# Bias matmuls replaced by a bias in the PSUM evacuation, a third load slot in weight preparation, and a moved norm matmul

## The chip, the cores and the metric

One Trainium2 chip, eight cores. Every core runs the same program on its own two of the 16 sequences, and the cores do not exchange data. The time is that of the slowest core, in microseconds (us), for one execution.

## What is computed

One transformer layer for `t` of shape 16 x 4096 x 1024 in float32. Cut to what matters:

```python
xn  = layernorm(x)
qkv = xn @ W_qkv.T + b_qkv            # 3072 = Q, K, V of 1024 each; b_qkv has 3072 values
att = softmax(Q @ K.T / 32) @ V       # one head of 1024
x   = x + layernorm(att)
h   = silu(xn2 @ wg.T) * (xn2 @ wu.T) # xn2 = layernorm(x); wg, wu 3072 x 1024 int32 / 127
x   = x + layernorm(h @ wd.T)         # wd 1024 x 3072 int32 / 127
```

## The kernel before

The program emits every engine's instructions in a hand-written order, with semaphore waits between them. `P.em(engine, fn, waits, inc)` appends one; an engine runs its own in that order. Its parts are:

*Weight preparation* (`prep_chunk`, L170). All four weight matrices are loaded in 26 chunks (18 of 2 MB, 8 of 1.5 MB) by SP, cast to bf16 by ScalarE (L191), transposed by TensorE (L197), copied out of PSUM by VectorE (L203) and stored to HBM by GpSimd's queue (L210). There are two load slots in `varena` and two store slots `sstg`: chunk `ch` can be loaded once the casts of `ch - 2` are done, and staged once the store of `ch - 2` has landed. At its end the bias row is loaded and cast into `bq`, which lies in `kbufs` (L120, L237). A fence over all engines follows.

*Then, for each of two sequences:* phase 1 projects Q, K and V, phase 2 is attention, phase 3 the MLP. A fence ends the sequence.

*Phase 1* runs over 8 groups `g` of 512 tokens. The layer norm of a token tile (L134 to L143, L318) alternates between VectorE and ScalarE; those of group g+1 are emitted after QK steps 8, 10, 12 and 14 of group g, in the same two queues as the evacuations. A group then is:
- four tiles transposed into `LNxT` (L346, L354);
- 16 QK steps `e_`: eight matmuls of 128 x 512 into one of two `pqk` banks (L372) and a ninth, one-row matmul that adds the bias (`bq` slice as the stationary operand, `ones_row` moving, L376); ScalarE evacuates to bf16 (L385), VectorE squares (L396);
- after step 7 eight matmuls sum the squares of Q (`pqn`, L412), after step 15 those of K (`pkn`, L430), for a bound on the scores;
- V: four tiles x two halves, eight matmuls each into one of two `pv` banks (L458), a one-row bias matmul (L463) and ScalarE's evacuation into `varena` (L470);
- GpSimd's queue stores Q and K to HBM (L477, L487).

The weights come in six sets of 1 MB a group, w0 to w5, into two halves of `wbufs` (`wload`, L282). w0 to w3 serve four QK steps each. w0 and w1 are issued when the V stage before is done, w2 to w5 when the set two before has been used: w2 after step 3, w3 after step 7, w4 after step 11, w5 after step 15. V's first halves use w4, its second halves w5. All are issued by SP, in order; the four `t` tiles of group g+1 (L303, 512 KB each) are issued just behind w2. Q's store is issued after step 7.

*Phase 2* begins with a small chain on ScalarE, VectorE and TensorE (L493 to L511) that turns the norms into `bias_exp`. Blocks of 512 queries follow; K comes in sets of four tiles into two halves of `kbufs` (L645). The first K set of block 0 waits for the end of V, as `kbufs` holds the bias row (L649).

*At sequence 1's start* the bias row is loaded and cast again (L246 to L255), and the first four `t` loads wait for it (`bq_gate`).

## Time and profile before

| | |
|---|---|
| two timed executions | 5873.38 and 6515.4 us, median 6194.39 |
| the profiled execution | 5885.66 us; span of the slowest core 5884.1 |
| spans of the eight cores | 5850.5 to 5884.1 us |
| weight preparation | 0 to 284 us |
| phase 1, sequence 0 and 1 | 284 to 878 and 3079 to 3671 us |
| TensorE busy | 5042.6 us, 86% |
| VectorE, ScalarE, GpSimd busy | 1303.3, 1210.0, 221.3 us |
| mean granted TensorE clock | 0.93 |

The profile is one execution recorded by the hardware on its slowest core (core 2). Times in its rows are microseconds from the start of the span, means of one instruction are nanoseconds. PE is TensorE's matmuls, PEld its weight loads, DVE VectorE, ACT ScalarE, POOL GpSimd, SP the engine that issues loads. L372 is line 372 of the kernel. "[1.61 <-DMA ...]" behind an instruction is the idle time of its engine before it, and what ended it. Some matmul records are missing, so that x7 can stand for eight. A matmul's shown duration has its pipeline's tail in it; the distance of starts tells the rate.

### The profile page before, as it was taken

To read this page: it belongs to the slowest core of one execution; us is meant where nothing else is said; L and a number is where in the kernel's file an instruction comes from. 1 tells how busy PE (TensorE), PEld (TensorE's weight loads), DVE (VectorE), ACT (ScalarE), POOL (GpSimd) and SP (SyncE) were. 2 spreads that over 40 slices of the span, in tenths; PEclk is the share of its full clock that TensorE was granted. 3 is DMA by queue.
4 is the path that set the end of the run, shared out by engine and by line. 5 is a ranking of instruction groups with operands and counts; after the bars stand their busy time and mean duration, and the time that the engine had idled before them with its cause. 6 is when DMAs were issued, how large, how long until landed. Compare 5 with 4: busy or idle time off the path is not lost.

```text
span 5884.1 us, 59117 instructions; the slowest of 8 cores (5850.5 to 5884.1 us)
## 1 busy us (share of the span) xinstructions
PE 5042.6 (86%) x23063; PEld 2243.1 (38%) x23492; DVE 1303.3 (22%) x1908; ACT 1210.0 (21%) x1951; POOL 221.3 (4%) x310
## 2 busy tenths in 40 slices
PE   3388889999999698989888888999999969898988
PEld 2233334444444344444433333444444434444443
DVE  2232221111111222223223222111111122232322
ACT  3322222222122121212112222222212212121211
POOL 1100000000000000000000000000000000000000
PEclk6598999999999799999998999999999979999999
DMA  9855554444333533343325555444433353334332
GB/s 276 254 142 143 143 140 108 110 112 110 93 100 97 125 86 93 90 99 104 66 78 151 143 143 142 105 112 108 115 93 101 93 129 86 93 86 97 105 71 72
DMA packets 735510, 679.18 MB, mean 115 GB/s; under 512 B 409602, under 2 KB 655362, under 8 KB 734210
## 3 DMA queue, kind: packets, MB, share of 16 engines
q1 hardware_dynamic: 699748, 549.52, 38.4%
q0 software_dynamic: 35488, 125.85, 5.9%
q8 instruction: 191, 3.13, 0.2%
q14 instruction: 83, 0.68, 0.0%
HBM read 549.48 MB, written 125.83 MB: 115 GB/s over the span
## 4 chain that ended last, share of the span: by engine, by line
PE 75%; DMA 14%; DVE 4%; issue 3%; ACT 3%; SPq 0%; DVEq 0%; ACTq 0%; POOL 0%; POOLq 0%
PE s1pav L583 8%; PE s0pav L583 8%; PE s1pd L898 6%; PE s0pd L898 6%; PE s0psc L668 5%; PE s1psc L668 5%; DMA kbufs<-kscr 5%; PE s1pg L830 5%; PE s0pg L830 5%; PE s1pu L844 5%; PE s0pu L844 5%; DMA wbufs<-wqkvT 4%; PE s0pqk L372 4%; PE s1pqk L372 4%; PE s1pv L458 2%
## 5 line engine op out<-in xcount | busy, mean ns | idle before, releaser
L668 PE MATMUL s1psc<-qarena,kbufs 128*128 128x512 bf16 x2004 | 448.0, 380 | 40.7 <-DMA kbufs<-kscr 34.1
L668 PE MATMUL s0psc<-qarena,kbufs 128*128 128x512 bf16 x2004 | 447.2, 380 | 41.0 <-DMA kbufs<-kscr 31.2
L583 PE MATMUL s1pav<-varena,parena 128*128 128x512 bf16 x2005 | 456.8, 388 | 3.3 <-issue 1.4
L583 PE MATMUL s0pav<-varena,parena 128*128 128x512 bf16 x2005 | 450.4, 385 | 2.7 <-issue 0.6
L830 PE MATMUL s1pg<-varena,wbufs 128*128 128x512 bf16 x1504 | 353.0, 385 | 8.7 <-DVE varena L782 5.7
L830 PE MATMUL s0pg<-varena,wbufs 128*128 128x512 bf16 x1504 | 353.0, 385 | 8.7 <-DVE varena L782 5.7
L844 PE MATMUL s1pu<-varena,wbufs 128*128 128x512 bf16 x1504 | 344.8, 379 | 1.7
L844 PE MATMUL s0pu<-varena,wbufs 128*128 128x512 bf16 x1504 | 344.8, 379 | 1.7
L134 DVE BATCH_NORM_STATS2 stats<-evac 128x6 f32<-128x512 f32 x128 | 88.9, 694 | 1104.8 <-ACT evac L597 719.1
L668 PEld LDWEIGHTS s1psc<-qarena,kbufs 128*128 128x128 bf16 x2048 | 198.3, 98 | 289.0 <-issue 56.6
L668 PEld LDWEIGHTS s0psc<-qarena,kbufs 128*128 128x128 bf16 x2048 | 198.2, 98 | 288.6 <-issue 56.4
L583 PEld LDWEIGHTS s1pav<-varena,parena 128*128 128x128 bf16 x2048 | 203.9, 100 | 252.5 <-issue 22.3
L372 PE MATMUL s0pqk<-parena,wbufs 128*128 128x512 bf16 x992 | 254.3, 398 | 49.7 <-DMA wbufs<-wqkvT 42.9
L583 PEld LDWEIGHTS s0pav<-varena,parena 128*128 128x128 bf16 x2048 | 202.2, 99 | 247.2 <-issue 13.2
L372 PE MATMUL s1pqk<-parena,wbufs 128*128 128x512 bf16 x993 | 255.7, 400 | 43.9 <-DMA wbufs<-wqkvT 40.5
L197 PE MATMUL ptr<-ident,lnout 128*128 128x128 bf16 x768 | 92.2, 303 | 184.0 <-ACT lnout L191 141.0
L898 PE MATMUL s1pd<-varena,parena 128*128 128x512 bf16 x1008 | 232.3, 381 | 7.4 <-DVE qarena L864 6.5
L898 PE MATMUL s0pd<-varena,parena 128*128 128x512 bf16 x1008 | 230.6, 379 | 7.0 <-DVE qarena L864 6.2
L677 ACT ACTIVATE parena<-s1psc,bias_exp 128x512 bf16<-128x512 f32 x256 | 175.1, 687 | 293.8 <-PE s1psc L668 293.8
L677 ACT ACTIVATE parena<-s0psc,bias_exp 128x512 bf16<-128x512 f32 x256 | 175.1, 687 | 293.0 <-PE s0psc L668 293.0
L830 PEld LDWEIGHTS s1pg<-varena,wbufs 128*128 128x128 bf16 x1536 | 151.6, 99 | 195.2 <-issue 21.3
L830 PEld LDWEIGHTS s0pg<-varena,wbufs 128*128 128x128 bf16 x1536 | 151.5, 99 | 195.2 <-issue 21.4
(126 smaller groups left out, 4408.0 us busy)
## 6 DMA issues: line engine op xcount, KB each, us to landing
wbufs<-wgT SPq DMA_DIRECT2D x96, 512.0 KB, 4.4
wbufs<-wuT SPq DMA_DIRECT2D x96, 512.0 KB, 6.2
xa<-t SPq DMA_DIRECT2D x64, 512.0 KB, 7.2
xb<-t SPq DMA_DIRECT2D x64, 512.0 KB, 5.4
xnew<-evac POOLq DMA_DIRECT2D x64, 512.0 KB, 4.6
xa<-xnew SPq DMA_DIRECT2D x64, 512.0 KB, 7.7
xb<-xnew SPq DMA_DIRECT2D x64, 512.0 KB, 4.4
out<-evac POOLq DMA_DIRECT2D x64, 512.0 KB, 4.8
```

The costliest lines, as they stand in the source:

```text
L134: e.bn_stats(out=o, in_=i), waits=list(extra_waits), inc="dve")
L197: e.transpose(out=o, in_=i, identity=ident[:]),
L372: e.matmul(out=o, lhsT=l, rhs=rr, start=st, stop=False),
L458: e.matmul(out=o, lhsT=l, rhs=rr, start=st, stop=False),
L583: e.matmul(out=o, lhsT=l, rhs=rr, start=st, stop=sp),
L668: e.matmul(out=o, lhsT=l, rhs=rr, start=st, stop=sp),
L677: e.activation(out=o, in_=i, func=AF.Exp, scale=ISQ, bias=bias_exp[:]),
L830: e.matmul(out=o, lhsT=l, rhs=rr, start=st, stop=sp),
L844: e.matmul(out=o, lhsT=l, rhs=rr, start=st, stop=sp),
L898: e.matmul(out=o, lhsT=l, rhs=rr, start=st, stop=sp),
```

## The change

The bias matmuls are gone. At the end of weight preparation the Q and K part of the bias is loaded as 16 x 128, transposed into `bqT` (128 x 16), and the V part is spread over 128 partitions into `bvrep` by two matmuls. Q's and K's evacuation on ScalarE becomes an Identity activation with a per-partition bias; V's moves to VectorE as an add with `bvrep`. The bias is not loaded again for sequence 1, no `t` load waits for it, and the first K load doesn't wait for V. The K norm's matmuls and its two small VectorE operations move from behind step 15 to behind the two halves of V's first tile. Weight preparation has three load slots, and its two store slots move from `varena` to `qarena`.

```diff
-    bq = kbufs[0:1, 0:E3]
+    bqT = sb("bqT", [128, 16], F32)
+    bvrep = sb("bvrep", [128, 1024], F32)
...
-    sstg = varena[:, 32768 - 16384: 32768]
+    sstg = qarena
...
-        slot = ch % 2
+        slot = ch % 3
         lsrc = vf32[:, slot * 4096: slot * 4096 + nsub * 1024]
         if in_i32:
             lsrc = lsrc.bitcast(I32)
-        lsem = ("wla", "wlb")[slot]
+        lsem = ("wla", "wlb", "qa")[slot]
         lt = (lsem, P.em(syn, lambda e, o=lsrc.rearrange(
                   "p (c d) -> p c d", c=nsub), i=src_ap:
                   e.dma_start(out=o, in_=i),
-                  waits=[("act", cast_tok.get(ch - 2)), ("pool", init_tok)],
+                  waits=[("act", cast_tok.get(ch - 3)), ("pool", init_tok)],
                   inc=lsem, amt=16))
         ld_tok[ch] = lt
-        stg = sstg[:, slot * 4096: slot * 4096 + nsub * 1024]
+        stg = sstg[:, (ch % 2) * 4096: (ch % 2) * 4096 + nsub * 1024]
...
-        psem = ("psa", "psb")[slot]
+        psem = ("psa", "psb")[ch % 2]
...
-    bqf = parena.bitcast(F32)[0:1, 0:E3]
-    bl = ("misc", P.em(syn, lambda e: e.dma_start(out=bqf,
-                                         in_=bqkv.rearrange("(a e) -> a e", a=1)),
-              inc="misc", amt=16))
-    bq_tok = P.em(act, lambda e: e.activation(out=bq[:], in_=bqf, func=AF.Copy),
-                  waits=[bl], inc="act")
+    pbv = [pps.enter_context(nc.psum_tensor(f"pbv{i}", [128, 512], F32))
+           for i in range(2)]
+    bstg = parena.bitcast(F32)[0:16, 0:128]
+    bstg2 = parena.bitcast(F32)[0:1, 1024:2048]
+    b16 = lnout[0:16, 0:128]
+    b16v = lnout[0:1, 1024:2048]
+    bl = ("misc", P.em(syn, lambda e: e.dma_start(
+        out=bstg, in_=bqkv[0:2048].rearrange("(c p) -> c p", p=128)),
+        inc="misc", amt=16))
+    blv = ("misc", P.em(syn, lambda e: e.dma_start(
+        out=bstg2, in_=bqkv[2048:3072].rearrange("(a e) -> a e", a=1)),
+        inc="misc", amt=16))
+    c1 = P.em(act, lambda e: e.activation(out=b16, in_=bstg, func=AF.Copy),
+              waits=[blv, ("pe", tr_tok[sub_i[0] - 2]), ("pool", init_tok)],
+              inc="act")
+    c2 = P.em(act, lambda e: e.activation(out=b16v, in_=bstg2, func=AF.Copy),
+              waits=[blv, ("pe", tr_tok[sub_i[0] - 1])], inc="act")
+    bt = P.em(pe, lambda e: e.transpose(out=ptr[0][:, 0:16], in_=b16,
+                                        identity=ident[0:16, 0:16]),
+              waits=[("act", c1), ("dve", cp_tok[sub_i[0] - 2])], inc="pe")
+    bm0 = P.em(pe, lambda e: e.matmul(out=pbv[0][:, :], lhsT=ones_row[0:1, 0:128],
+                                      rhs=b16v[:, 0:512], start=True, stop=True),
+               waits=[("act", c2)], inc="pe")
+    bm1 = P.em(pe, lambda e: e.matmul(out=pbv[1][:, :], lhsT=ones_row[0:1, 0:128],
+                                      rhs=b16v[:, 512:1024], start=True, stop=True),
+               inc="pe")
+    bq_tok = P.em(act, lambda e: e.activation(out=bqT[:], in_=ptr[0][:, 0:16].bitcast(F32)[:, 0:16] if False else ptr[0][:, 0:16], func=AF.Copy),
+                  waits=[("pe", bt)], inc="act")
+    P.em(act, lambda e: e.activation(out=bvrep[:, 0:512], in_=pbv[0][:, :],
+                                     func=AF.Copy), waits=[("pe", bm1)])
+    bq_tok = P.em(act, lambda e: e.activation(out=bvrep[:, 512:1024],
+                                              in_=pbv[1][:, :], func=AF.Copy),
+                  inc="act")
...
-        if s > 0:
-            bqf2 = xa.bitcast(F32)[0:1, 0:E3]
-            bl2 = ("misc", P.em(syn, lambda e, o=bqf2,
-                                in2=bqkv.rearrange("(a e) -> a e", a=1):
-                                e.dma_start(out=o, in_=in2),
-                                inc="misc", amt=16))
-            bq_tok = P.em(act, lambda e, o=bq, i=bqf2:
-                          e.activation(out=o, in_=i, func=AF.Copy),
-                          waits=[bl2], inc="act")
-            bq_gate = ("act", bq_tok)
-        else:
-            bq_gate = ("act", bq_tok)
+        bq_gate = None
...
-                waits=[apply_tok.get(tile - 4), dbg_gate.get(tile - 2),
-                       bq_gate if tile < 4 else None],
+                waits=[apply_tok.get(tile - 4), dbg_gate.get(tile - 2)],
...
-                          ("act", bq_tok)]
+                          ("act", bq_tok if g == 0 else None)]
+                mmt = None
                 for c in range(8):
                     lhs = wv[:, (e_ % 4) * 1024 + c * 128:
                              (e_ % 4) * 1024 + (c + 1) * 128]
                     rhs = LNxT[:, c * 512:(c + 1) * 512]
-                    P.em(pe, lambda e, o=pqk[bank][:, :], l=lhs, rr=rhs, st=(c == 0):
-                         e.matmul(out=o, lhsT=l, rhs=rr, start=st, stop=False),
-                         waits=mwaits if c == 0 else ())
-                mmt = P.em(pe, lambda e, o=pqk[bank][:, :],
-                           l=bq[:, e_ * 128:(e_ + 1) * 128], rr=ones_row[:, :]:
-                           e.matmul(out=o, lhsT=l, rhs=rr, start=False, stop=True),
-                           inc="pe")
+                    mmt = P.em(pe, lambda e, o=pqk[bank][:, :], l=lhs, rr=rhs,
+                               st=(c == 0), sp=(c == 7):
+                               e.matmul(out=o, lhsT=l, rhs=rr, start=st, stop=sp),
+                               waits=mwaits if c == 0 else (),
+                               inc="pe" if c == 7 else None)
                 if e_ < 8:
                     dst = QTst[:, e_ * 512:(e_ + 1) * 512]
                     stage_free = qt_dma.get(g - 1)
                 else:
                     dst = Kst[:, (e_ - 8) * 512:(e_ - 8 + 1) * 512]
                     stage_free = kscr_dma.get(g - 1)
-                et = P.em(act, lambda e, o=dst, i=pqk[bank][:, :]:
-                          e.activation(out=o, in_=i, func=AF.Copy),
+                et = P.em(act, lambda e, o=dst, i=pqk[bank][:, :],
+                          b=bqT[:, e_: e_ + 1]:
+                          e.activation(out=o, in_=i, func=AF.Identity, bias=b),
                           waits=[("pe", mmt), stage_free], inc="act")
...
-                if e_ == 15:
-                    tok = None
-                    for c in range(8):
-                        tok = P.em(pe, lambda e, o=pkn[:, :],
...
-                              ("act", vql_tok.get((g, j - 1, hf),
-                                                  vql_tok.get((g - 1, 3, hf)))),
-                              ("act", bq_tok)]
+                              ("dve", vql_tok.get((g, j - 1, hf),
+                                                  vql_tok.get((g - 1, 3, hf))))]
+                    mmt = None
                     for c in range(8):
                         lhs = LNxT[:, c * 512 + j * 128: c * 512 + (j + 1) * 128]
-                        P.em(pe, lambda e, o=pv[hf][:, :], l=lhs,
-                             rr=wv4[:, :, c, :], st=(c == 0):
-                             e.matmul(out=o, lhsT=l, rhs=rr, start=st, stop=False),
-                             waits=mwaits if c == 0 else ())
-                    mmt = P.em(pe, lambda e, o=pv[hf][:, :],
-                               l=ones_row[:, 0:128],
-                               rr=bq[:, 2048 + hf * 512: 2048 + (hf + 1) * 512]:
-                               e.matmul(out=o, lhsT=l, rhs=rr,
-                                        start=False, stop=True),
-                               inc="pe")
+                        mmt = P.em(pe, lambda e, o=pv[hf][:, :], l=lhs,
+                                   rr=wv4[:, :, c, :], st=(c == 0), sp=(c == 7):
+                                   e.matmul(out=o, lhsT=l, rhs=rr,
+                                            start=st, stop=sp),
+                                   waits=mwaits if c == 0 else (),
+                                   inc="pe" if c == 7 else None)
                     dst = varena[:, tile * 1024 + hf * 512:
                                  tile * 1024 + (hf + 1) * 512]
                     vql_tok[(g, j, hf)] = P.em(
-                        act, lambda e, o=dst, i=pv[hf][:, :]:
-                        e.activation(out=o, in_=i, func=AF.Copy),
-                        waits=[("pe", mmt)], inc="act")
+                        dve, lambda e, o=dst, i=pv[hf][:, :],
+                        b=bvrep[:, hf * 512:(hf + 1) * 512]:
+                        e.tensor_add(out=o, in0=i, in1=b),
+                        waits=[("pe", mmt)], inc="dve")
+                if j == 0:
+                        tok = None
+                        for c in range(8):
+                            tok = P.em(pe, lambda e, o=pkn[:, :],
+                                       rr=q2s[:, c * 512:(c + 1) * 512],
+                                       st=(c == 0), sp=(c == 7):
+                                       e.matmul(out=o, lhsT=ones_col[:], rhs=rr,
+                                                start=st, stop=sp),
+                                       waits=[("dve", sq2_tok[(g, 15)]),
+                                              ("dve", kmax_tok.get(g - 1))],
+                                       inc="pe" if c == 7 else None)
+                        kn_tok[g] = tok
+                        rm = P.em(dve, lambda e, i=pkn[:, :]: e.reduce_max(
+                            out=tiny[:, 6:7], in_=i, axis=AX.X),
+                            waits=[("pe", tok)], inc="dve")
+                        kmax_tok[g] = P.em(dve, lambda e: e.tensor_max(
+                            out=tiny[:, 1:2], in0=tiny[:, 1:2], in1=tiny[:, 6:7]),
+                            waits=[("dve", rm)], inc="dve")
...
-                  waits=[("dve", nb_), ("act", vql_tok[(NG1 - 1, 3, 0)])],
+                  waits=[("dve", nb_), ("dve", vql_tok[(NG1 - 1, 3, 0)])],
...
-                               ("ksr", ks_relay[si]),
-                               ("pe", vlast_tok[NG1 - 1]
-                                if (b == 0 and si == 0) else None)],
+                               ("ksr", ks_relay[si])],
```

## Rows read from the trace of the kernel before

**Rows 1.** The page's chain that ended last, by engine, share of the span.
```profile
PE 75%; DMA 14%; DVE 4%; issue 3%; ACT 3%; SPq 0%; DVEq 0%; ACTq 0%; POOL 0%; POOLq 0%
```
**Rows 2.** Groups by line: bias matmuls. Columns: count | busy us, mean ns | idle before.
```profile
L376 PE MATMUL s0pqk<-ones_row,kbufs 1*128 1x512 bf16 x128 | 50.4, 394 | 1.2
L463 PE MATMUL s0pv<-kbufs,ones_row 1*128 1x512 bf16 x64 | 24.8, 388 | 0.0
```
**Rows 3.** Timeline, PE: two bias matmuls in phase 1, one score set. Columns: start, us.
```profile
311.52 0.39 PE L376 MATMUL s0pqk<-ones_row,kbufs 1*128 1x512 bf16 x1
...
313.67 0.39 PE L376 MATMUL s0pqk<-ones_row,kbufs 1*128 1x512 bf16 x1
...
918.69 7.07 PE L668 MATMUL s0psc<-qarena,kbufs 128*128 128x512 bf16 x31 [0.88 <-ACT parena L677]
```
**Rows 4.** Timeline, PE, group 6 of sequence 0 and the start of group 7.
```profile
741.82 3.19 PE L372 MATMUL s0pqk<-parena,wbufs 128*128 128x512 bf16 x7 [5.22 <-DMA wbufs<-wqkvT]
...
762.38 1.89 PE L412 MATMUL s0pqn<-q2s,ones_col 128*1 128x512 bf16 x8 [1.37 <-DVE q2s L396]
...
774.48 1.89 PE L372 MATMUL s0pqk<-parena,wbufs 128*128 128x512 bf16 x8 [1.61 <-DMA wbufs<-wqkvT]
...
785.86 1.89 PE L430 MATMUL s0pkn<-q2s,ones_col 128*1 128x512 bf16 x8 [2.73 <-DVE q2s L396]
...
790.42 1.89 PE L458 MATMUL s0pv<-wbufs,parena 128*128 128x512 bf16 x8 [0.52 <-DMA wbufs<-wqkvT]
...
813.74 3.19 PE L372 MATMUL s0pqk<-parena,wbufs 128*128 128x512 bf16 x7 [5.52 <-DMA wbufs<-wqkvT]
```
**Rows 5.** Chain that ended last, weight loads in order of time. Columns: issue, us.
```profile
761.15 13.08 DMA wbufs<-wqkvT
783.27 7.02 DMA wbufs<-wqkvT
...
3413.13 11.92 DMA wbufs<-wqkvT
```
**Rows 6.** Windows of group 6: each engine's busy time, granted clock, DMA share, GB/s.
```profile
742.00:747.00 5.00, 5.00 (x14) 1.48 (x13) 0.43 (x1) 0.60 (x1) 0.00 (x0) 0.57 0.61 119
754.00:772.00 18.00, 16.53 (x70) 6.10 (x71) 6.00 (x14) 4.57 (x9) 0.91 (x1) 1.00 0.97 289
...
794.00:807.00 13.00, 12.52 (x65) 4.94 (x63) 0.82 (x2) 3.58 (x6) 0.00 (x0) 1.00 0.01 2
```
**Rows 7.** Timeline, PE: the K norm of group 0.
```profile
349.95 3.16 PE L430 MATMUL s0pkn<-q2s,ones_col 128*1 128x512 bf16 x8 [2.73 <-DVE q2s L396]
```
**Rows 8.** Timeline, SP: the issue of the `t` tiles in group 6.
```profile
753.32 5.73 SPq L303 DMA_DIRECT2D xa<-t  x4
```
**Rows 9.** Timeline, PE: from the last V matmul to the first scores.
```profile
880.36 0.35 PE L507 MATMUL s0pv<-tiny,ones_rf 1*128 1x1 f32 x2 [2.00 <-DVE tiny L504]
887.10 15.05 PE L668 MATMUL s0psc<-qarena,kbufs 128*128 128x512 bf16 x62 [6.40 <-DMA kbufs<-kscr]
```
**Rows 10.** Groups by line: an add, two evacuations, table loads at the Ln line.
```profile
L925 DVE TENSOR_TENSOR evac<-dn,xb 128x1024 f32<-128x1024 f32 x64 | 78.4, 1226 | 12.1 <-DVE dn L920 12.1
...
L677 ACT ACTIVATE parena<-s0psc,bias_exp 128x512 bf16<-128x512 f32 x256 | 175.1, 687 | 293.0 <-PE s0psc L668 293.0
...
L385 ACT ACTIVATE parena<-s0pqk 128x512 bf16<-128x512 f32 x128 | 75.9, 593 | 247.7 <-PE s0pqk L376 247.7
...
L140 ACT ACT_TABLE_LOAD x26 | 33.4, 1283 | 88.7 <-DVE stats L138 88.7
```
**Rows 11.** Chain that ended last, start of sequence 1. Columns: start, us.
```profile
3078.90 1.94 DMA xa<-bqkv
3080.92 2.77 ACT kbufs L253
```
**Rows 12.** Windows of weight preparation, columns as in rows 6.
```profile
0.00:40.00 40.00, 11.59 (x96) 9.38 (x96) 8.20 (x12) 13.33 (x13) 5.12 (x15) 1.00 0.80 244
40.00:220.00 180.00, 63.23 (x520) 50.37 (x520) 43.36 (x63) 66.41 (x66) 28.29 (x17) 0.56 0.97 287
220.00:284.00 64.00, 17.42 (x152) 14.20 (x152) 13.92 (x21) 21.07 (x19) 9.94 (x7) 0.53 0.75 222
```

More of the change, by code:

```diff
@@ L423, in build_nc @@
                         waits=[("dve", rm)], inc="dve")
-                if e_ == 15:
-                    tok = None
-                    for c in range(8):
-                        tok = P.em(pe, lambda e, o=pkn[:, :],
-                                   rr=q2s[:, c * 512:(c + 1) * 512],
-                                   st=(c == 0), sp=(c == 7):
-                                   e.matmul(out=o, lhsT=ones_col[:], rhs=rr,
-                                            start=st, stop=sp),
-                                   waits=[("dve", sq2_tok[(g, 15)]),
-                                          ("dve", kmax_tok.get(g - 1))],
-                                   inc="pe" if c == 7 else None)
-                    kn_tok[g] = tok
-                    rm = P.em(dve, lambda e, i=pkn[:, :]: e.reduce_max(
-                        out=tiny[:, 6:7], in_=i, axis=AX.X),
-                        waits=[("pe", tok)], inc="dve")
-                    kmax_tok[g] = P.em(dve, lambda e: e.tensor_max(
-                        out=tiny[:, 1:2], in0=tiny[:, 1:2], in1=tiny[:, 6:7]),
-                        waits=[("dve", rm)], inc="dve")
             for j in range(4):
```

## The prediction

> **What bounds the kernel now.** I read the chain that ended last first: three quarters of the span are TensorE's own work and a seventh is DMA [rows 1]. TensorE is the engine to follow, but only where it is not waiting. The groups by line then give the size of what is removed: 384 one-row bias matmuls, 256 into `pqk` and 128 into `pv`, each shown at about 0.39 us [rows 2]. Busy time is not what one costs, since matmuls overlap, so I take starts. In projection phase one `e_` step of eight matmuls plus bias repeats every 2.15 us (311.52 to 313.67), while 32 matmuls of the score phase, which have no bias, take 7.07 us with a tail of 0.38, that is 0.216 us each [rows 3]. Eight of them are 1.73 us, so one bias matmul costs 0.42 us, twice a full matmul: both changes between one-row and 128-row weights break the overlap. In all 384 x 0.42 = 162 us of TensorE time go. The question is how much of that was free to go, and that is read from one group of the projection phase.
>
> I call T the first QK matmul of group 6 of sequence 0, at 741.82 us [rows 4]; w0 to w5 are its six 1 MB weight loads into two buffers. Each of w2 to w5 starts when the set two before it is used up. Today: T+19.2 QK step 7 ends; T+22.4 step 8 starts after the Q norm; step 12 waits 1.61 us for w3; step 15 ends at T+41.3; 2.73 us of wait, the K norm (1.8 us), the first V half; the second V half waits for w5 until T+48.6; V ends 7 x 2.15 us later, T+63.8; the next group starts at 813.74, T+71.9 [rows 4]. The loads: w3 goes out at 761.15 and takes 13.08 us (11.92 in a group of sequence 1), w5 goes out at 783.27 and takes 7.02 us [rows 5]. Between 754 and 772 us the DMA engines are 97% busy (w2, four tiles of `t`, w3, the Q store); in the V stage they are idle [rows 6]. So w3 is bound by bandwidth and w5 by latency, and neither gets shorter with faster matmuls.
>
> The clock: the granted clock is 0.57 of full in the first 5 us of the group [rows 6], after 5.2 us of idle PE. After 2.73 us of idle the K norm took 1.89 us in this group but 3.16 us in group 0 [rows 4, 7], so such a wait sometimes leads to half clock; after 1.37 us [rows 4] it did not here. Half clock is 0.43 us a matmul, so 5 us of it lose 2.5 us of matmuls without bias (today 2.0, the steps' gaps hide in it).
>
> **The change, part by part.** *Groups 0 to 6, both sequences (14).* New times: step 3 ends T+9.4 (11.7 matmuls in the slow 5 us, 20.3 at 0.216), step 7 T+16.3, step 8 starts 3.2 us later as now, T+19.5, step 11 ends T+26.4. Bounds of w3: its own duration, T+16.3 + 11.9 = T+28.2; or bandwidth, 20.9 us after the `t` loads start (753.32 to 774.23 today [rows 5, 8]), which is T+10.2 + 20.9 = T+31.1. I take the middle, so step 12 starts at T+29.9: a wait of 3.5 us. Four steps 6.9 us, and the price of the clock after such a wait between 0 and 2.5, taken 1.3 as it is near the 2.73 us waits: step 15 ends at T+38.1. Now the moved K norm: it no longer fills the wait for w5. w5 is there 7.3 us after step 15 as today, T+45.4, and only one V half (1.7 us) stands before it, so PE idles 5.6 us, a wait as long as those with a sure low clock. Then seven V halves 12.1, the K norm 1.8, low clock 2.5: V ends T+61.8. The way to the next group stays 8.1 us (w0 can be loaded only when V ends): T+69.9 against 71.9. That is 2.0 us a group, 28 us in all. With both prices at their good end (w3 at 28.2, no low clock after it) it is 4.6 a group, 64 us; at their bad end (31.3 for step 12, 2.5) the group takes 72.5 us, a loss of 8 us in all.
>
> *Group 7 (2).* No `t` is loaded, so w3 is there in time: step 15 ends T+33.3, V starts in earnest at T+40.6, V ends T+57.0, against 878.36 - 813.74 = 64.6 [rows 4, 9]. I take 6 of those 7.6 us for each, since w5 shares the engines with Q and now K loads: 12 us, bounds 8 and 15.
>
> *V's evacuation on VectorE, Q and K's with a bias.* The trace has no such add; the f32 add of 1024 columns took 1.23 us, so 512 lie between half of that, 0.61, and all of it, and I take 0.65 us, as the columns are half. ScalarE's copy took 0.59, its activation with bias and scale 0.69 [rows 10]; one with a bias alone lies between. All are hidden behind a 1.73 us V half or step; VectorE is otherwise empty in the V stage. Even at 1.23 us an add fits into the V half beside it. I cost it at nothing; without that cover it would be 0.65 us for each of 128 adds, 83 us.
>
> *Projection to scores (2).* Without the bias row in `kbufs`, the first two K loads no longer wait for V and land under it. Today V's end 878.36, the softmax bias matmul 880.36, then 6.40 us until K at 887.10, and the first 64 score matmuls take 15.05 us where 64 x 0.216 is 13.8 [rows 9]. What stays is the chain 2.0 + 0.35 + about 1.4 us for ScalarE's copy of `bias_exp` with its two hand-overs (an estimate, twice an activation of 0.69): 3.8 instead of 8.7, and part of the 1.1 us of clock. 5.5 each, 11 us (8 to 15). The third K load still waits for a buffer.
>
> *Start of sequence 1.* The reload of the bias goes: 1.94 us DMA and 2.77 us ScalarE, in series ahead of `t` [rows 11]. 5 us.
>
> *Weight preparation.* Three load slots instead of two. DMA engines are busy 80% in the first 40 us, 97% up to 220 us and 75% at the end [rows 12]. A third load fills the first hole: 0.20 x 40 = 8 us, less the 3 us before any load, 5 us. In the middle it brings nothing. At the end the two store slots, untouched, limit it. Lower bound of the gain 0; upper 5 plus 0.25 x 64 = 16, 21 us. I take 5. The new transposes and copies of the bias lie under the last store.
>
> Sum: 28 + 12 + 11 + 5 + 5 = 61 us off 5885.7 us (the profiled execution, span 5884.1): **5825 us**, -1.0%. Bounds: -8 + 8 + 8 + 5 + 0 = 13 to 64 + 15 + 15 + 5 + 21 = 120 us. The median of the two runs shown, 6194.39, is a mean of two far apart, 5873.38 and 6515.4; the profiled execution is near the lower and I forecast on its level.
>
> The Trainium skill (TensorE: Matmul & The Clock Gate, back-to-back issue gap) gives a 512-column matmul about 216 ns and says that the number of rows of a weight load does not matter. The spacing without bias agrees; the 0.42 us of the bias matmul does not. By the page's figure 83 us would go raw: V and steps 12 to 15 would save 2.4 us a group less, the 14 groups would lose 6 us instead of gaining 28, the last ones would gain 2 instead of 12, and the sum would be 17 us, 5869 us.
>
> **Rivals.** (a) *Both new waits cost the full clock price.* 3.5 us is longer than the waits that were sometimes free and shorter than those never free. With w3 also at its bandwidth bound: groups +8 instead of -28, 5861 us. For it: the 97%; against: w3 took 1.2 us less in sequence 1. The same page (HAM oscillation) says that DMA waits between bursts of matmuls bring every burst back to half clock; the trace agrees for the 5.2 us waits and not for 1.37 us. By the page alone with my middle w3, 1.2 us a group more, 5842 us.
> (b) *TensorE-bound after all*: loads come as early as the matmuls ask. Then all 162 us go, with 11 + 5 + 5: 5703 us. For it: step 12 waited for w3 only 1.61 us. Against: the 97% and the latency of w5.
> (c) *Slower*: ScalarE must switch function tables between the new biased evacuation and Ln/Exp of the next layer norms. A load is 1.283 us and there were 26 at the Ln line [rows 10], too few for one at each layer norm, so Copy shares a table with them; nothing in the trace shows that Identity does. If not: two loads at each of four layer norms, 10.3 us a group, less the 3.5 us of wait it hides in: 6.8 x 14 = 95 us, 5920 us. It decides once a layer norm loses more than 2 us. The Trainium skill (ScalarE: Activation LUTs, Table sets) counts identity among the functions that every set holds, which speaks against (c).
> (d) *Preparation gains its bound*, 21 instead of 5: 5809 us, inside my range.
>
> **Chances.** My case with (d) 0.62, (a) 0.21, (b) 0.07, (c) 0.06, others 0.04. The range 5775 to 5875 us takes in the bounds 120 and 13 us and holds the first two. A measurement of this kernel can tell about 2%, 118 us. Faster by more: (b) and one of the others, 0.08. Slower by more (6003 us): 0.03, as (c) alone stays below. Within: 0.89.
>
> **What would show it.** QK steps 1.73 us apart at full clock; step 12 waiting 2 to 5 us for w3 in groups 0 to 6 and hardly in 7; about 5.6 us of wait for w5 before the second V half of every group, and a low clock after it; groups 68 to 72 us apart; TensorE's 384 one-row matmuls gone but its idle time up by about 100 us; no table load between layer norms; scores within 4 us of V's end; first `t` load right after the fence. Wrong would be a wait for w5 below 3 us, groups 65 us apart, or V halves spaced by VectorE.

## The result and the profile after

The changed kernel took 5811.04 us in its profiled execution, 74.6 us less than the one before (5885.66). Over all executions the medians are 5938.89 us (11 runs, 5805.93 to 6361.35) against 6342.86 us (10 runs); they say little, since in about half of the executions of every kernel the cores of one die or of both ran at a lower granted clock, and only the others are compared in this document, except for the length of weight preparation, for which all profiled ones are used. Those compared lie, for the changed kernel, between 5805.93 and 5812.79 us, and the ratio to before is 0.9878 [0.9858, 0.9898]: 1.2% less time, which is under the 2% that a measurement of this kernel can tell.

Part of the 74.6 us belongs to the profiled execution of before. Measured again later, next to the experiments, before took 5858.55 to 5875.37 us in eleven of the twelve executions compared (5923.94 in the other). In the first of these series it took 5867.6 us in the mean of three, and the changed kernel with two load slots 5808.9 us in the mean of two, ratio 0.9896 [0.9842, 0.995]: 59 us, near the 61 of the forecast.

The page of after, in order: the span, the engines' busy time, the chain that ended last by engine.

```profile
span 5809.5 us, 58400 instructions; the slowest of 8 cores (5776.5 to 5809.5 us)
...
PE 4930.9 (85%) x22697; PEld 2243.9 (39%) x23111; DVE 1387.4 (24%) x2036; ACT 1151.7 (20%) x1826; POOL 221.2 (4%) x310
...
PE 71%; DMA 16%; DVE 4%; issue 3%; ACT 3%; SPq 1%; DVEq 0%; ACTq 0%; POOL 0%; POOLq 0%
```

TensorE's share of the chain fell from 75 to 71%, DMA's rose from 14 to 16% [rows 1]: the time was partly handed from matmuls to weight loads. The groups by line of after say where (columns as in rows 2):

```profile
L390 PE MATMUL s0pqk<-parena,wbufs 128*128 128x512 bf16 x1000 | 248.2, 408 | 72.0 <-DMA wbufs<-wqkvT 59.6 <-ACT parena L401 8.7 <-DVE parena L370 1.4
L390 PE MATMUL s1pqk<-parena,wbufs 128*128 128x512 bf16 x1000 | 248.0, 407 | 68.3 <-DMA wbufs<-wqkvT 51.6 <-ACT parena L401 13.5 <-ACT stats L141 1.2
...
L455 PE MATMUL s0pv<-wbufs,parena 128*128 128x512 bf16 x512 | 127.7, 409 | 44.8 <-DMA wbufs<-wqkvT 44.8
...
L401 ACT ACTIVATE parena<-s0pqk,bqT 128x512 bf16<-128x512 f32 x128 | 86.4, 683 | 376.2 <-PE s0pqk L390 376.2
...
L464 DVE TENSOR_TENSOR varena<-s0pv,bvrep 128x512 bf16<-128x512 f32 x64 | 44.2, 691 | 110.3 <-PE s0pv L455 110.3
...
L141 ACT ACT_TABLE_LOAD x26 | 33.4, 1283 | 88.6 <-DVE stats L139 88.6
```

The same two groups of sequence 0 before:

```profile
L372 PE MATMUL s0pqk<-parena,wbufs 128*128 128x512 bf16 x992 | 254.3, 398 | 49.7 <-DMA wbufs<-wqkvT 42.9 <-ACT parena L385 1.9 <-ACT stats L143 1.5
...
L458 PE MATMUL s0pv<-wbufs,parena 128*128 128x512 bf16 x512 | 125.7, 390 | 4.9 <-DMA wbufs<-wqkvT 4.9
```

The V matmuls, which waited 4.9 us in all for weights before, wait 44.8 now; the QK matmuls wait 59.6 us for weights, 42.9 before. V's add on VectorE is hidden: no V matmul waits for it. ScalarE's evacuation of Q and K is not: the QK matmuls wait for it (L401) 8.7 us in sequence 0 and 13.5 in sequence 1, where 1.9 and 0 stood before. The table loads at the layer norm's line are still 26 [rows 10].

By stages, each line the profiled execution of before and of after (from starts in the two traces), and what the prediction's sum had for it:

| stage | before, us | after, us | gained | forecast |
|---|---|---|---|---|
| weight preparation, to the first `t` load | 284.2 | 275.5 | 8.7 | 5 |
| groups 0 to 6, both sequences | 1010.6 | 991.6 | 19.0 | 28 |
| group 7 to the first scores, both | 145.4 | 117.9 | 27.5 | 12 + 11 |
| phase 3 of sequence 0 and start of sequence 1 | 1156.3 | 1151.9 | 4.4 | 5 |
| attention, both | 2128.0 | 2115.8 | 12.2 | 0 |
| first `t` load to first QK, and the last phase 3 | 1159.6 | 1156.8 | 2.8 | 0 |
| sum | 5884.1 | 5809.5 | 74.6 | 61 |

Phase 1, from its first QK matmul to the first scores, in four sums that I worked out of the traces (the length; TensorE's idle time in waits over 0.15 us; the time in which it worked at half clock, 1.2 of 2.4 GHz; and "work", the length less the idle time and half of the half-clock time), in us, sequence 0 / sequence 1:

| kernel | length | idle | at half clock | work |
|---|---|---|---|---|
| before | 580.9 / 575.0 | 96.0 / 88.7 | 56.1 / 59.2 | 456.9 / 456.8 |
| after | 557.0 / 552.5 | 133.1 / 130.0 | 86.2 / 82.4 | 380.7 / 381.4 |

The work removed is 76.2 + 75.4 = 151.6 us, near the 162 us foreseen for the bias matmuls. Of it 78 us came back as idle time and 27 us (half of 30.1 + 23.2) as half clock; 46 us stayed. Of the idle time 20 us are waits for ScalarE's evacuations (22.2 against 1.9).

One group shows how. This is PE's timeline in group 6 of sequence 0 of after, the group of rows 4:

```profile
725.24 16.12 PE L390 MATMUL s0pqk<-parena,wbufs 128*128 128x512 bf16 x62 [4.93 <-DMA wbufs<-wqkvT]
742.82 1.89 PE L427 MATMUL s0pqn<-q2s,ones_col 128*1 128x512 bf16 x8 [1.46 <-DVE q2s L412]
...
751.10 1.89 PE L390 MATMUL s0pqk<-parena,wbufs 128*128 128x512 bf16 x7 [1.11 <-ACT parena L401]
755.35 5.34 PE L390 MATMUL s0pqk<-parena,wbufs 128*128 128x512 bf16 x24 [2.36 <-DMA wbufs<-wqkvT]
761.46 1.89 PE L390 MATMUL s0pqk<-parena,wbufs 128*128 128x512 bf16 x8 [0.77 <-ACT parena L401]
763.19 1.89 PE L455 MATMUL s0pv<-wbufs,parena 128*128 128x512 bf16 x8
770.63 3.57 PE L455 MATMUL s0pv<-wbufs,parena 128*128 128x512 bf16 x8 [5.56 <-DMA wbufs<-wqkvT]
774.14 1.99 PE L472 MATMUL s0pkn<-q2s,ones_col 128*1 128x512 bf16 x8
...
795.38 4.84 PE L390 MATMUL s0pqk<-parena,wbufs 128*128 128x512 bf16 x15 [6.04 <-DMA wbufs<-wqkvT]
```

and these are its loads w3, w5 and the next w0, from the chain that ended last, with the window around w3 (columns of rows 6):

```profile
741.86 13.25 DMA wbufs<-wqkvT
763.49 7.01 DMA wbufs<-wqkvT
786.73 8.03 DMA wbufs<-wqkvT
```

```profile
738.00:755.00 17.00, 12.32 (x54) 4.91 (x54) 7.42 (x16) 5.48 (x11) 0.91 (x1) 1.00 1.02 306
```

w3 went out 16.6 us after T (19.3 before) and took 13.25 us (13.08 before [rows 5]) with the DMA engines fully busy; w5 took 7.01 (7.02). Neither got shorter, so TensorE, which is now done with w2 sooner, waits at step 12 (755.35), and the second V half waits 5.56 us where 0.52 us stood before. The eight matmuls behind that wait are shown with 3.57 us, half clock, where the eight of the first V half have 1.89. Steps 11 and 15 (751.10 and 761.46) wait 1.11 and 0.77 us for ScalarE's evacuation.

### The profile page after: what moved, and what is told of

It reads as the page before. It is cut to its first block, busy times and chain, and to the rows that moved or that the text cites. A ratio compares the mean times of both kernels' runs of the same rounds, so it can differ in the third digit from the quotient of the medians.

```text
span 5809.5 us, 58400 instructions; the slowest of 8 cores (5776.5 to 5809.5 us)
## 1 busy us (share of the span) xinstructions
PE 4930.9 (85%) x22697; PEld 2243.9 (39%) x23111; DVE 1387.4 (24%) x2036; ACT 1151.7 (20%) x1826; POOL 221.2 (4%) x310
## 4 chain that ended last, share of the span: by engine, by line
PE 71%; DMA 16%; DVE 4%; issue 3%; ACT 3%; SPq 1%; DVEq 0%; ACTq 0%; POOL 0%; POOLq 0%
PE s0pav L596 8%; PE s1pav L596 8%; DMA wbufs<-wqkvT 6%; PE s0pd L909 6%; PE s1pd L909 6%; PE s0psc L679 6%; DMA kbufs<-kscr 5%; PE s0pg L841 5%; PE s1pg L841 5%; PE s0pu L855 5%; PE s1pu L855 5%; PE s1psc L679 5%; PE s0pqk L390 3%; PE s1pqk L390 3%; PE s0pv L455 2%
## 5 line engine op out<-in xcount | busy, mean ns | idle before, releaser
L679 PE MATMUL s0psc<-qarena,kbufs 128*128 128x512 bf16 x2004 | 446.3, 379 | 26.0 <-DMA kbufs<-kscr 16.3
L596 PE MATMUL s0pav<-varena,parena 128*128 128x512 bf16 x2005 | 458.5, 389 | 3.3 <-issue 1.2
L390 PE MATMUL s0pqk<-parena,wbufs 128*128 128x512 bf16 x1000 | 248.2, 408 | 72.0 <-DMA wbufs<-wqkvT 59.6
L596 PEld LDWEIGHTS s1pav<-varena,parena 128*128 128x128 bf16 x2048 | 204.1, 100 | 252.9 <-issue 23.2
```

What stands on the lines that cost most here:

```text
L390: e.matmul(out=o, lhsT=l, rhs=rr, start=st, stop=sp),
L596: e.matmul(out=o, lhsT=l, rhs=rr, start=st, stop=sp),
L679: e.matmul(out=o, lhsT=l, rhs=rr, start=st, stop=sp),
```

## Experiments

**The K norm back behind step 15.** Of the change everything is kept but the K norm's move.

```diff
+                if e_ == 15:
+                    ... (K norm: 8 matmuls, reduce_max, tensor_max)
...
-                if j == 0:
-                    ... (the same)
```

> The changed kernel with one part undone: the K norm's matmuls and its two VectorE operations stand behind QK step 15 again, ahead of V. Theory (the second V half waits for w5, 7.3 us after step 15, whatever stands before it): the norm's 1.8 us go back into that wait, V ends 1.8 us earlier in each of 16 groups, and the wait of 5.6 us falls apart into about 2.7 and 1.1 us, so that the low clock after it costs 1.3 instead of 2.5 us: 3 us a group, 48 us in all, 5763 us. Rival (the move paid, since it took the wait of 2.73 us for the last square out of TensorE's way): 2.7 us a group come back, 5854 us.

Measured: 5751.4 and 5750.2 us, ratio to before 0.9797 [0.9755, 0.9839]. PE's timeline of this kernel in the group that starts at 621.37:

```profile
657.67 1.89 PE L390 MATMUL s0pqk<-parena,wbufs 128*128 128x512 bf16 x8 [0.77 <-ACT parena L401]
662.29 1.89 PE L446 MATMUL s0pkn<-q2s,ones_col 128*1 128x512 bf16 x8 [2.73 <-DVE q2s L412]
664.11 1.90 PE L474 MATMUL s0pv<-wbufs,parena 128*128 128x512 bf16 x8
666.72 12.25 PE L474 MATMUL s0pv<-wbufs,parena 128*128 128x512 bf16 x56 [0.71 <-DMA wbufs<-wqkvT]
```

From the start of step 15 to the second V half it is 666.72 - 657.67 = 9.05 us here and 770.63 - 761.46 = 9.17 us in after: w5 sets this moment in both. But here the K norm lies in front of it, and in after behind it, with the half clock that follows 5.56 us of idle. The V stage from then on: 678.80 - 666.72 = 12.1 us against 786.43 - 770.63 = 15.8 us (to the first transposes, 678.80 and 786.43 in the two timelines). That is 3.7 us in this group. Over all 16, phase 1 is 524.8 / 532.0 us long here and 557.0 / 552.5 in after, 52.7 us or 3.3 a group; the kernels differ by about 60, and the rest of it lies outside phase 1, where single executions differ by as much. So the move of the K norm cost over 50 us, more than the whole change gained in phase 1 (46).

**Idle matmuls in the wait for w5.** 22 matmuls of `ones_col` with `LNxT` into the `pkn` bank, whose result is overwritten, behind the first V half.

```diff
+                    if j == 0 and hf == 0:
+                        for f_ in range(22):
+                            P.em(pe, ... e.matmul(out=pkn, lhsT=ones_col[:], rhs=rr,
+                                          start=True, stop=True), ...)
```

> The changed kernel with 22 idle matmuls (one column of ones by 512 columns, into the K norm's bank, overwritten after) behind the first V half of each group, in the wait of 5.6 us for w5. They take 4.8 us at full clock and compute nothing that is used. Theory (a wait of 5.6 us is followed by about 5 us at half clock, which costs 2.5 us): the wait stays as long but TensorE is busy in it, and the clock stays up: 2 us a group, 32 us in all, 5779 us. Rival (the clock behind the wait costs nothing, or the fillers themselves run at half clock and come out of the wait late): 5811 us or more.

Measured: 5782.4 and 5780.6 us, about 29 us below after. Phase 1: length 540.3 / 540.9, idle 94.0 / 94.8, half clock 48.8 / 47.5, work 421.9 / 422.3. PE's timeline of this kernel:

```profile
675.02 4.91 PE L470 MATMUL s0pkn<-parena,ones_col 128*1 128x512 bf16 x22
680.48 1.89 PE L455 MATMUL s0pv<-wbufs,parena 128*128 128x512 bf16 x8 [0.55 <-DMA wbufs<-wqkvT]
```

The second V half comes no sooner, 680.48 - 671.48 = 9.0 us after step 15's start, but what follows runs at full clock. The clock's share of the wait for w5 is thus about 2 us a group, which the prediction had as 2.5; what is left of the 3.3 us a group is near the 1.8 us of the K norm's own matmuls.

**Four weight buffers instead of two.** `xb` and `evac`, idle in phase 1, become buffers 3 and 4, so that each load is issued two sets earlier. In after and in before:

```diff
+        def wbuf(gs):
+            i = gs % 4
+            if i < 2:
+                return wbufs[:, i * 4096:(i + 1) * 4096]
+            return (xb, evac)[i - 2].bitcast(BF16)[:, 0:4096]
...
-                    wload(g, e_ // 4 + 2)
+                    wload(gs + 4)
```

> The changed kernel with four buffers for the weight sets of phase 1 instead of two: xb and evac, idle in that phase, hold the third and fourth, and a set is loaded as soon as the set four before it is used up. Theory (the waits for w0, w3 and w5 and the low clock behind them eat what the bias matmuls gave): the waits go, a group takes TensorE's own 49 us and 3 us of layer norms in the way, 52 instead of 71, and the kernel about 290 us less, 5520 us (5480 to 5600). Rival (DMA bandwidth is the bound, not the two buffers): groups stay above 65 us, 5720 us or more.

> The kernel before, with bias matmuls, the K norm behind step 15 and two slots in preparation, with the same four buffers. Theory (a bias matmul costs 0.42 us of TensorE and its removal is hidden only by the loads): with loads out of the way the change is worth its full 384 x 0.42 = 162 us plus 9 in preparation and 10 at the borders, so this kernel is about 180 us above the changed one with four buffers, near 5700 us. Rival (a bias matmul costs 0.216 us like any other): 83 + 19 us above it, near 5620 us.

Measured: after with four buffers 5565.7, 5562.7, 5557.0 us, ratio to before 0.9472 [0.9429, 0.9514]; before with four buffers 5769.3, 5766.2 us, ratio 0.9826 [0.9784, 0.9868]. PE's timeline of a whole group of the first:

```profile
508.53 15.66 PE L393 MATMUL s0pqk<-parena,wbufs 128*128 128x512 bf16 x64 [1.16 <-DVE parena L374]
525.65 1.89 PE L430 MATMUL s0pqn<-q2s,ones_col 128*1 128x512 bf16 x8 [1.46 <-DVE q2s L415]
527.47 5.35 PE L393 MATMUL s0pqk<-parena,xb 128*128 128x512 bf16 x24
...
543.34 3.62 PE L457 MATMUL s0pv<-wbufs,parena 128*128 128x512 bf16 x16
546.88 1.89 PE L474 MATMUL s0pkn<-q2s,ones_col 128*1 128x512 bf16 x8
548.71 10.53 PE L457 MATMUL s0pv<-wbufs,parena 128*128 128x512 bf16 x48
```

No wait for a weight load is left, and its groups by line have none over the whole sequence (the line of the first and third set):

```profile
L393 PE MATMUL s0pqk<-parena,wbufs 128*128 128x512 bf16 x512 | 120.0, 395 | 9.1 <-ACT parena L404 4.6 <-DVE parena L374 4.5
```

The next group starts at 563.14, 54.6 us later, and between 507 and 562 us the DMA engines are 73% busy. Phase 1: with the change 433.3 / 433.8 us, work 382.4 / 382.3; without it 527.3 / 523.0, work 458.5 / 458.9. So the same change that brings 74 us with two buffers brings 5767.8 - 5564.2 = 204 us with four (spans of the profiled executions). This is the main evidence for the theory of the forecast, that the loads' return times and not the matmuls set a group; the 204 are somewhat above the 180 expected. Phase 1 gives 94.0 + 89.2 = 183 of them, its way to the scores included: 153 of work, 4 of half clock and 26 of idle time (50.7 / 50.2 without the change, 37.3 / 37.6 with it). The last is the balance of three things: 41 us of waits in front of the K norm and 12 us for the first K loads are gone, and TensorE waits 21 us for ScalarE's evacuations, 0 without the change. So moving the K norm may well pay with four buffers, where it cost with two; no run has its old place with four.

**Three buffers** (only `xb` added).

> The changed kernel with three buffers for the weight sets instead of two or four (xb is the third). Theory (what hurts is that a set's load can start only when the set two before it is done, not the bandwidth): with three, w0 of the next group and w5 are asked for one set earlier and are there in time, and the kernel is within 20 us of that with four, 5570 to 5590 us. Rival (a set behind the four t tiles needs more than 12 us, and three buffers still leave TensorE waiting for it): 2 to 5 us a group remain, 5600 to 5650 us.

Measured: 5557.6 us, one execution, as with four. By it one more load in flight is enough.

**What a ninth matmul costs when nothing waits.** The kernel with four buffers gets a ninth matmul of zeros in every QK step and V half, with 128 rows or with one; the result is not altered.

```diff
+    zt = sb("zt", [128, 128], BF16)          # zeros
...
+                mmt = P.em(pe, lambda e, o=pqk[bank][:, :], l=zt[0:ROWS, :],
+                           rr=LNxT[0:ROWS, 0:512]:
+                           e.matmul(out=o, lhsT=l, rhs=rr, start=False, stop=True),
+                           inc="pe")
```

> The changed kernel with four weight buffers (5565.7 us), with a ninth matmul added to each of the 384 accumulations of phase 1: stationary operand 128 rows x 128 columns of zeros, moving operand 128 x 512. It adds nothing to the result. Theory (what doubled the price of a bias matmul was the change between one row and 128 rows): it costs 0.216 us, 83 us in all, 5649 us, steps 1.94 us apart. Rival (a ninth matmul with another kind of operand costs 0.42 us whatever its rows): 5728 us, 2.15 us apart.

> As the run before, but the ninth matmul has one row (a row of 128 zeros stationary, one row of 512 moving), as the bias matmuls had. Theory: 0.42 us each, steps 2.15 us apart, 162 us in all, 5728 us. Rival (rows don't matter): same as with 128 rows, 5649 us.

Measured, one execution each: 5628.2 us with 128 rows and 5689.2 us with one row, against 5557 to 5566 without. PE's timelines, first with 128 rows, then with one (its core 0):

```profile
300.37 0.38 PE L399 MATMUL s0pqk<-parena,zt 128*128 128x512 bf16 x1
...
302.31 0.38 PE L399 MATMUL s0pqk<-parena,zt 128*128 128x512 bf16 x1
```

```profile
301.86 0.38 PE L399 MATMUL s0pqk<-parena,zt 1*128 1x512 bf16 x1
...
304.01 0.38 PE L399 MATMUL s0pqk<-parena,zt 1*128 1x512 bf16 x1
```

The same durations are shown, but the steps are 1.94 and 2.15 us apart, where eight matmuls alone take 1.73: the ninth costs 0.21 us with 128 rows and 0.42 us with one. The second is the spacing of before [rows 3]. Over 384 of them these are 81 and 161 us; the time rose by about 65 and 126 us. The difference is seen in phase 1. With 128 rows its work rose by 81 us, while the half-clock time fell from 27.3 / 27.8 to 8.0 / 19.4 us, worth half of that, 14 us, and the idle time by 10. With one row (core 0) the work rose by 153 us, while the half-clock time fell to 9.7 / 14.6 us, worth 15, and the idle time by 22. Nearly all of the idle time that went was waiting for ScalarE's evacuations: 21.1 us with steps of 1.73 us, 11.5 with 1.94 and 0.7 with 2.15, the same Identity activation in all three. So it is the shorter step that ScalarE, which does layer norms between the evacuations, cannot keep up with.

**Weight preparation.** The change without the third slot; before with the two store slots moved to `qarena`; before with that and the third slot. These and before were run again for the spread.

```diff
-        slot = ch % 3          # the first: back to ch % 2, cast_tok.get(ch - 2)
+        slot = ch % 2
...
-    sstg = varena[:, 32768 - 16384: 32768]     # the second, in before
+    sstg = qarena
```

> The changed kernel with two load slots in weight preparation, as before; all else stays. Theory (the third slot gave the 8.7 us by which the first t load is earlier, all of it in the first 40 us and the last 60): the first t load at 284 us instead of 275.5, 5820 us. Rival (the 8.7 us came from elsewhere, such as the bias row that no longer has its cast at the end): first t load stays at 275.5, 5811 us.

> The kernel before with only the change in weight preparation: three load slots, and the two store slots in qarena instead of varena. Phase 1 keeps its bias matmuls and the bias row. Theory one (the third slot, or the new place of the store slots, gave the 8.7 us by which the first t load is earlier): first t load near 270 us, 5872 us. Theory two (the difference is in the bias row's cast, or it is the spread between executions): first t load at 275 to 284 us as in the two profiles of the old preparation, 5881 us.

> The kernel before with only the two store slots moved from varena to qarena; two load slots. If the place of the store slots is what counts, the first t load comes near 265 us, as in the changed kernel with two slots, 5870 us. If the third slot counts, it stays at 275 to 284 us, 5881 us. If neither does, this kernel, the one with three slots and the one before lie within 5 us of each other on the mean of the cores.

> The changed kernel with two load slots in weight preparation, profiled a second time. Its first profile had the first t load at 265.0 us on the mean of the cores, 257.7 on one die. Theory (the third slot is worth about 8 us and that one die was a stray of this execution): mean 272 to 276 us. Rival (two slots are as good as three once the store slots are in qarena and the bias has its new cast): 264 to 267 us.

> The kernel before, unchanged, profiled a second time for the spread of weight preparation between executions. Theory (the 283.4 us of its first profile, mean of the cores, is the upper end of a spread): first t load at 274 to 277 us. Rival (the old place of the store slots costs 8 us more): 280 to 284 us.

> The kernel before with the store slots in qarena and two load slots, profiled again. If its 274.6 us for the first t load (mean of the cores) is its own, it comes at 273 to 276 us again; if two slots are as good as three, near 266.

> The kernel before with the whole new weight preparation (three load slots), profiled again. If the third slot is worth 8 us in this program, 265 to 268 us for the first t load; if the difference to the run before it is the spread of an execution, anything between 264 and 276.

> The changed kernel with two load slots, profiled a third time. After 265.0 and 267.1 us: if two slots with the new bias cast are as good as three, 264 to 268 us again; if those were strays, 272 to 276 us.

Measured: without the third slot 5803.7, 5814.0 and, again, 5801.9 us (after: 5806 to 5813), not the 5820 of the theory. Before with its store slots moved 5861.1, 5864.0, 5862.3, 5859.2 and 5861.75 us, ratio 0.9979 [0.9919, 1.0039]; with the third slot too 5855.35 us, from its second run; its first, before's second and the third of after with two slots gave only their preparation. The start of the first `t` load, the mean over the eight cores of one profiled execution, is a finer measure (each value is one execution of one kernel with this preparation):

| kernel | two load slots | three load slots |
|---|---|---|
| with the bias handling of before | 283.4 (before), 274.9, 274.6, 275.7, 273.7 | 266.5, 267.0 |
| with that of after | 265.0, 267.1, 270.7 | 270.9 (after), 264.1, 264.3, 266.7, 264.8, 266.5, 266.4 |

The second profiles of before (275.7), of before with its store slots moved (273.7), of that with three slots (267.0) and of after with two (267.1) came where one of the two expectations had them; the third of after with two, 270.7, fell between both. In before the third slot is worth 7 to 8 us; in after it is worth nothing that these runs can tell, though executions of one kernel differ by 6 to 8 us (265.0 to 270.7; before 283.4 and 275.7). With two slots the kernels with the new bias handling are 7 us sooner in the mean than those with the old (283.4 left out), which is about what the third slot brings alone, and the two don't add up. The end of preparation, where the bias is handled, does not make that difference: the last weight load already goes out at 245.4 to 246.5 us (mean over the cores; 253.2 in the profile of before) with the old and at 237.4 to 242.9 with the new, and up to there the instructions are the same. The cast of the bias row was hidden, too: in the profile of before it ends at 274.1 us, the last store is issued at 277.5 and the first `t` load at 284.2. What made the kernels with the new bias handling faster up to there is open. In the windows view of after the first 40 us are now 92% full and the middle 98% (80 and 97% before [rows 12]):

```profile
0.00:40.00 40.00, 12.51 (x104) 10.15 (x104) 8.20 (x12) 15.33 (x15) 5.69 (x15) 1.00 0.92 276
40.00:220.00 180.00, 61.87 (x515) 49.66 (x515) 43.87 (x65) 65.47 (x65) 27.72 (x17) 0.72 0.98 299
```

A third load in flight mostly lengthened each: the median 2 MB load took 27 us where it had taken 17.8.

## Where the prediction was right, and the step that failed

The mechanism was right: in groups 0 to 6 TensorE waits for w3 and w5 and most of the bias matmuls' time comes back as waits and half clock. The step that failed is "Four steps 6.9 us" with the evacuations "at nothing": TensorE waits for ScalarE's evacuations, and groups 0 to 6 gained 19 us, not 28. The times compared, 5806 to 5813 us, lie in the range and 12 to 19 us below 5825. The median over all executions, 5938.89 us, lies above it: "I forecast on its level" left the forecast without any term for the executions above that of the profile. The sum was 61 and 74.6 us were gained, but that the two are as near as that is partly luck: the 9 us too many in groups 0 to 6 are outweighed by 12.2 us in attention, in which the change has hardly a part, 4.5 at the border to the scores, 3.7 in preparation and 2.8 in places without a term. The sentence that the range takes in the bound of 120 us is off: 5885.7 - 120 is 5766, below 5775. Step by step:

*The timetable of group 6* came out within 0.6 us at nearly every point: step 7's end T+16.1 (16.3 forecast), step 12's start T+30.1 (29.9), step 15's end T+38.0 (38.1), the wait for w5 5.56 (5.6) up to T+45.4 (45.4), V's end T+61.2 (61.8), next group T+70.1 (69.9). Step 12's wait was 2.36 us and not 3.5, since step 11 had already waited 1.11 us for ScalarE, whose evacuation came late among the layer norms. The two bounds for w3 (T+28.2 and T+31.1) were both right as a pair: it landed at T+28.3 to T+31.3 over the groups.

*Groups 0 to 6: 28 forecast, 19 measured. The failed step in numbers.* In the mean of the 14 groups step 12 starts at T+30.1 (29.9 forecast), V follows 8.64 us later (8.2), w5's V half 7.47 after that (7.3) and the next group 24.6 later (24.5): a period of 70.8 us, 0.9 above the forecast, while before's mean was 72.2, 0.3 above the 71.9 taken. The largest part is the stretch from step 12 to V. Its matmuls are the 6.9 us of the forecast and its half clock 2.35 us, a price of 1.2 where 1.3 was taken; the rest is mostly 0.46 us of waiting for ScalarE's evacuations, 6 us over the 14 groups, where the forecast had nothing. The price of the clock was right as a mean of two kinds of groups: in nine of the ten that waited for w3 TensorE then ran at half clock for about 3.4 us (5.9 in one), and in group 6 of sequence 0, after 2.36 us, and in the four that waited at step 12 for something else, 1.2 to 2.1 us, it did not. So rival (a), the full price after both waits, came true for w5's wait and half true for w3's. The Trainium skill (TensorE: Matmul & The Clock Gate, HAM oscillation) has every burst behind a DMA wait of its kernel come back at half clock, a price of 2.5 here by the forecast; the trace agrees for the waits for w5 and for nine of the ten for w3. The periods, 68.4 to 73.8 us, are spread wider than the forecast's one number.

*The wait for w5* was foreseen with its cause, 5.35 to 5.87 us in groups 0 to 6, and the experiment with the K norm moved back shows what moving it cost, 53 us in phase 1. The forecast held the move's effect inside the 2.0 us a group and never set it apart. Had it, its own timetable would have shown that this one part of the change costs a group (1.8 us of norm and part of the 2.5 us of clock) more than the whole change brings it.

*Group 7 and projection to scores: 23 forecast, 27.5 measured.* The chain was as described. PE's timeline of after:

```profile
852.91 0.35 PE L520 MATMUL s0pv<-tiny,ones_rf 1*128 1x1 f32 x2 [1.54 <-DVE tiny L517]
854.09 13.76 PE L679 MATMUL s0psc<-qarena,kbufs 128*128 128x512 bf16 x62 [0.84 <-ACT bias_exp L524]
```

The scores start 1.18 us after the softmax bias matmul, where 6.74 us stood before [rows 9] and 0.35 + 1.4 were estimated, and the first 64 take 13.8 us, at full clock. ScalarE's copy with its two hand-overs took 0.84 us, not 1.4. In group 7 w5 landed within 7.0 to 7.4 us although Q and K loads ran, so the 1.6 us a group taken off there were too many.

*Start of sequence 1: 5 forecast, 4.4 measured.* In the chain of after the `t` load follows the last store at once:

```profile
3038.99 2.88 DMA out<-evac
3042.04 3.56 DMA xa<-t
```

*Preparation: 5 forecast, 8.7 measured*, inside its bounds, but not for the reason given: by the table above the third slot brings nothing in this kernel that the runs can tell, and what does is open. That the bias's transposes and copies lie under the last store is so: in the trace of after they end at 270.8 us, and the first `t` load is issued at 275.5.

*Idle time of TensorE up by about 100 us* was foreseen; it was up by 78 in phase 1.

*The evacuations* were costed at nothing, which held for V's and failed for Q's and K's. VectorE's add took 691 ns (0.65 was taken), under a V half of 1.73 us, with VectorE otherwise nearly empty there. ScalarE's took 683 ns, also under a step of 1.73 us, but ScalarE has the layer norms between the evacuations, and with two `pqk` banks TensorE waited for it 22.2 us in all. The waits in front of step 11 are hidden where w3 is later still; those in front of step 15 are not.

*Attention, 12 us, was not forecast.* A little of it is in the first block, which has 0 / 2.7 us of half clock instead of 2.6 / 4.3. The rest is not the change's by any run here: over eleven profiled executions of these kernels the same stage of one sequence took 1051.4 to 1067.6 us, with and without the change.

*The rivals.* (b), TensorE-bound, fell for two buffers and was the way it went as soon as the loads were out of the way. (c), table switches, fell: the layer norm's line still has 26 table loads. The page it leaned on agrees: the Trainium skill (ScalarE: Activation LUTs, Table sets) counts identity among the functions that every set holds. The Trainium skill's 0.216 us for a 512-column matmul, whatever the rows of its weights (TensorE: Matmul & The Clock Gate, back-to-back issue gap and LDWEIGHTS), holds for the ninth matmul of 128 rows, 0.21 us, and fails for that of one row, 0.42 us; weighing the row over the page was right, and by the page the sum would have come out 44 us worse than it was forecast. The same section gives 216 ns as the spacing of an isolated matmul and about 131 ns in a stream of weight loads and matmuls; the streams here run at 216 [rows 3], and the measurement decides.

## What to carry to other kernels

Work taken off the busiest engine is worth what lies between it and the next load's return, so follow one period with its loads before counting instructions: here 152 us of TensorE work gave 46 us of phase 1, and 183 once more buffers had been found in tiles that lay idle. Before moving work past a wait, ask whether it was filling that wait: eight matmuls moved to the other side of one cost 3.3 us a group. An evacuation that is shorter than a step is not hidden by that alone, if its engine has other work in the same queue. And a matmul whose weights have another number of rows than its neighbours' can cost twice what its shown duration suggests; read the distance of starts.

## What the hardware showed beyond what was expected

- A one-row matmul between 128-row ones costs 0.42 us and a 128-row one 0.21, with the same 0.38 us shown for both.
- TensorE's granted clock was at half after each of the waits of 4.1 to 6 us in phase 1, after some of those of 2.73 us in before, and after none of those of 1.46 us in after. 22 matmuls of no use in a 5.6 us wait kept it up and gave back about 29 us in 16 groups.
- One 1 MB weight load took 7.0 us alone and 13.25 us behind w2 and four `t` tiles; with the DMA engines 98% busy, a third 2 MB load in flight took the median load from 17.8 to 27 us.
- An Identity activation with a per-partition bias of 512 columns out of PSUM took 683 ns, a copy 593.
